# The general path of a ten-table embedding kernel: TensorE's 19 loop bodies become one loop over 199 tiles, and table 9 goes first

## The reference

```python
embs = [jnp.dot(x, w) for x, w in zip(xs, ws)]
emb_sum = embs[0]
q_emb = jnp.dot(xs[0] ** 2, ws[0] ** 2)
for i in range(1, len(xs)):
    emb_sum = emb_sum + embs[i]
    q_emb = q_emb + jnp.dot(xs[i] ** 2, ws[i] ** 2)
fm_ans = 0.5 * (emb_sum ** 2 - q_emb)
return jnp.concatenate([fm_ans] + embs, axis=-1)
```

## Time and profile before

| | us |
|---|---|
| median of 3 runs | 287.22 (287.17 to 287.44) |
| the profiled execution | 289.03 |
| its span | 287.3 |
| TensorE busy (matmul / weight load) | 218.8 / 154.5 |
| VectorE busy | 240.2 |
| ScalarE busy | 227.6 |
| GpSimd busy | 88.3 |
| moved by DMA | 113.90 MB, mean 396 GB/s |

### The profile page before, as it was taken

The page is one execution under the profiler, slowest core; times in us unless marked ns, Lnnn a source line. Parts: engine busy times, 40 slices in busy tenths (PEclk is TensorE's granted clock), DMA queues, the critical chain, the costliest instruction groups (busy, mean ns, idle before and its releaser), DMA issues.

```text
span 287.3 us, 2928 instructions
## 1 busy us (share of the span) xinstructions
PE 218.8 (76%) x878; PEld 154.5 (54%) x878; DVE 240.2 (84%) x236; ACT 227.6 (79%) x271; POOL 88.3 (31%) x68
## 2 busy tenths in 40 slices
PE   0459989999887888877887887887787888777760
PEld 0338757666555555555554554555555555555550
DVE  3742999999999998888889888988888898888960
ACT  0769999998987888788977877877877888787940
POOL 0442527326214304109224224314314304104000
PEclk9999999999999999999999999999999999999995
DMA  7999999999999999999999999999999999999932
GB/s 235 403 406 413 408 416 415 420 412 420 416 423 414 420 420 417 419 413 417 422 419 417 419 420 421 419 422 418 416 419 421 419 419 412 416 411 425 404 134 80
DMA packets 22419, 113.90 MB, mean 396 GB/s; under 512 B 3728, under 2 KB 4752, under 8 KB 10752
## 3 DMA queue, kind: packets, MB, share of 16 engines
q1 hardware_dynamic: 16976, 106.90, 90.5%
q10 hardware_dynamic: 5424, 6.79, 6.6%
HBM read 110.79 MB, written 2.88 MB: 396 GB/s over the span
## 4 chain that ended last, share of the span: by engine, by line
DMA 62%; issue 23%; DVE 6%; ACT 3%; PE 2%; POOL 1%; ACTq 1%; DVEq 0%; POOLq 0%
DMA x_ring<-in_x_dram 57%; DVE is_one L450 5%; DMA whole<-in_w_dram 5%; ACT is_set L287 2%; PE sums L376 1%; ACT turned L298 1%; POOL low L357 1%; PE sums L383 1%; DVE total L487 0%; ACT whole L280 0%; ACTq L267 0%; POOL high L355 0%; DVE results L490 0%; DVE results L493 0%; ACTq L274 0%
## 5 line engine op out<-in xcount | busy, mean ns | idle before, releaser
L450 DVE TENSOR_SCALAR_CACHE_REDUCE is_one<-x_ring 128x2048 uint8<-128x2048 f32 (+2 forms) x108 | 226.2, 2116 | 28.5 <-DMA x_ring<-in_x_dram 28.4
L287 ACT ACTIVATE is_set<-x_ring 128x2048 fp32r<-128x2048 uint32 (+2 forms) x108 | 192.1, 1783 | 37.1 <-DMA x_ring<-in_x_dram 37.0
L376 PE MATMUL sums<-is_set,low 128*128 128x512 f32 x398 | 135.3, 422 | 59.0 <-ACT is_set L287 52.2
L376 PE MATMUL sums<-is_set,high 128*128 128x512 f32 x398 | 126.2, 399 | 0.0
L376 PEld LDWEIGHTS sums<-is_set,low 128*128 128x128 f32 x398 | 68.7, 191 | 103.4 <-ACT is_set L287 53.8
L376 PEld LDWEIGHTS sums<-is_set,high 128*128 128x128 f32 x398 | 76.2, 191 | 17.8
L355 POOL CAST high<-whole 128x1024 fp32r<-128x1024 f32 (+5 forms) x31 | 27.0, 872 | 170.2 <-ACT whole L280 170.2
L357 POOL TENSOR_TENSOR low<-whole,high 128x1024 fp32r<-128x1024 f32 (+5 forms) x31 | 60.7, 1957 | 2.5
L287 ACT ACTIVATION_READ_ACCUMULATOR is_set<-x_ring 128x1 f32 (+1 forms) x108 | 20.6, 191 | 0.0
L280 ACT ACTIVATE whole<-whole 128x512 f32<-128x512 f32 (+5 forms) x31 | 16.7, 540 | 4.0 <-DMA whole<-in_w_dram 4.0
L383 PE MATMUL sums<-identity,turned 128*128 128x128 f32 x80 | 10.8, 280 | 0.8 <-ACT turned L328 0.8
(11 more groups left out here) (17 smaller groups left out, 3.7 us busy)
## 6 DMA issues: line engine op xcount, KB each, us to landing
x_ring<-in_x_dram SPq DMA_DIRECT2D x91, 1024.0 KB, 18.4
x_ring<-in_x_dram SPq DMA_DIRECT2D x16, 512.0 KB, 10.2
whole<-in_w_dram ACTq DMA_DIRECT2D x19, 256.0 KB, 7.4
out_dram<-results SPq DMA_DIRECT2D x10, 256.0 KB, 12.5
x_ring<-in_x_dram SPq DMA_DIRECT2D x1, 448.0 KB, 6.2
whole<-in_w_dram ACTq DMA_DIRECT2D x2, 192.0 KB, 5.6
whole<-in_w_dram ACTq DMA_DIRECT2D x2, 160.0 KB, 7.1
out_dram<-results ACTq DMA_DIRECT2D x1, 256.0 KB, 2.1
```

What stands on the lines that cost most here:

```text
L287: nc.scalar.activation(is_set[chunk.k % SETS][0:chunk.rows, 0:chunk.n * BATCH], x_of(chunk).bitcast(U32), ACT.Sign, accum_out=set_counts[0 ...
L376: last = nc.tensor.matmul(sums[:, summing(n, half), :], w, x[0:chunk.rows, at:at + HALF], start=first, stop=False, skip_group_check=True)
L450: nc.vector.tensor_scalar(is_one[chunk.k % 2][0:chunk.rows, 0:chunk.n * BATCH], x_of(chunk), 1.0, None, ALU.is_equal, ALU.add, accum_out=o ...
```

## The change

PE's general path becomes one loop over all 199 tiles, always with 128 rows. For that the last tile of a table with more than one is no longer cut to `TAIL` rows: SP loads the last 128 rows of `x` there (`x_end`, which overlaps the tile before), and places the weights so that the rows already done meet the zero rows of the padding; this takes one more DMA and one more wait on a new semaphore `gz_landed` in each of the nine tables. Table 9, with 112 rows and one tile, goes first, into a slot that DVE has set to zero, so that its missing rows are zero. DVE keeps its loops by table and works on 128 rows throughout. The usual path is as it was.

```diff
+G_ORDER = [9] + [t for t in range(NT) if t != 9]
...
-    x_tail = [x[P * (n - 1):P * (n - 1) + rows] for n, rows, x in zip(TILES, TAIL, xs)]
...
+        gz_landed = sem("gz_landed")
...
             with sp.If(odd != 0):
-                for t in range(NT):
-                    base = sum(TILES[:t])
-
-                    def load_tile(i, rows, x):
-
-                        sp.wait_ge(g_multiplied, base + i + 1)
-                        sp.dma_start(in_slot(0, BATCH)[0:rows], x).then_inc(gx_landed, 16)
-                        sp.dma_start(g_weights[:, 0, :], w_dram[t][:, bass.ds(i * D, D)]
-                                     ).then_inc(gw_landed, 16)
-
-                    if TILES[t] > 1:
-                        with sp.Fori(0, TILES[t] - 1) as i:
-                            load_tile(i, P, x_dram[t][:, bass.ds(i * BATCH, BATCH)])
-                    load_tile(TILES[t] - 1, TAIL[t], x_tail[t])
+                base = zeros = 0
+                for t in G_ORDER:
+                    end, rows = TILES[t] - 1, TAIL[t]
+                    if end:
+                        with sp.Fori(0, end) as i:
+
+                            sp.wait_ge(g_multiplied, base + i + 1)
+                            sp.dma_start(in_slot(0, BATCH), x_dram[t][:, bass.ds(i * BATCH, BATCH)]
+                                         ).then_inc(gx_landed, 16)
+                            sp.dma_start(g_weights[:, 0, :], w_dram[t][:, bass.ds(i * D, D)]
+                                         ).then_inc(gw_landed, 16)
+                    sp.wait_ge(g_multiplied, base + end + 1)
+                    sp.dma_start(in_slot(0, BATCH)[0:x_end[t].shape[0]], x_end[t]).then_inc(gx_landed, 16)
+                    w_end, before = w_dram[t][:, end * D:TILES[t] * D], P - rows if end else 0
+                    if before:
+
+                        sp.dma_start(g_weights[0:before, 0, :], w_end[rows:P]).then_inc(gz_landed, 16)
+                        zeros += 1
+                        sp.wait_ge(gz_landed, 16 * zeros)
+                    sp.dma_start(g_weights[before:P, 0, :], w_end[0:P - before]).then_inc(gw_landed, 16)
+                    base += TILES[t]
...
             with pe.If(odd != 0):
-                for t in range(NT):
-                    base = sum(TILES[:t])
-
-                    def multiply_tile(i, rows):
-                        pe.wait_ge(gx_landed, 16 * (base + i + 1))
-                        pe.wait_ge(gw_landed, 16 * (base + i + 1))
-                        pe.wait_ge(gx_ready, 2 * (base + i + 1))
-                        for b in range(NB):
...
-                    if TILES[t] > 1:
-                        with pe.Fori(0, TILES[t] - 1) as i:
-                            multiply_tile(i, P)
-                    multiply_tile(TILES[t] - 1, TAIL[t])
+                with pe.Fori(0, sum(TILES)) as i:
+                    pe.wait_ge(gx_landed, 16 * (i + 1))
+                    pe.wait_ge(gw_landed, 16 * (i + 1))
+                    pe.wait_ge(gx_ready, 2 * (i + 1))
+                    for b in range(NB):
+                        block_b = slice(b * P, (b + 1) * P)
+                        nc.tensor.matmul(sums[:, b, 0:D], in_slot(0, BATCH)[:, block_b],
+                                         g_weights[:, 0, :], start=True, stop=True,
+                                         skip_group_check=True)
+                        last = nc.tensor.matmul(sums[:, b, D:2 * D], in_slot(1, BATCH)[:, block_b],
+                                                g_weights[:, 1, :], start=False, stop=True,
+                                                skip_group_check=True)
+                    last.then_inc(g_multiplied, 1)
...
                 dve.wait_ge(x_multiplied, NCHUNKS)
+
+                g_link(nc.vector.memset(in_slot(0, BATCH), 0.0))
                 nc.vector.nop().then_inc(g_multiplied, 1)
...
-                for t in range(NT):
-                    base = sum(TILES[:t])
+                base = 0
+                for t in G_ORDER:
...
-                    def add_tile(i, rows):
+                    def add_tile(i):
...
-                            add_tile(i, P)
-                    add_tile(TILES[t] - 1, TAIL[t])
+                            add_tile(i)
+                    add_tile(TILES[t] - 1)
+                    base += TILES[t]
```

More of the change, by code:

```diff
@@ L507, in _ @@
                 dve.wait_ge(x_multiplied, NCHUNKS)
+                g_link(nc.vector.memset(in_slot(0, BATCH), 0.0))
                 nc.vector.nop().then_inc(g_multiplied, 1)
                 g_link(nc.vector.memset(total[:, :, :, :], 0.0))
-                for t in range(NT):
-                    base = sum(TILES[:t])
+                base = 0
+                for t in G_ORDER:
                     emb = results[:, t + 1, :, :]
                     g_link(nc.vector.memset(emb, 0.0))
-                    def add_tile(i, rows):
+                    def add_tile(i):
                         dve.wait_ge(gx_landed, 16 * (base + i + 1))
                         dve.wait_ge(gw_landed, 16 * (base + i + 1))
-                        x, w = in_slot(0, BATCH)[0:rows], g_weights[:, 0, :]
-                        nc.vector.tensor_tensor(in_slot(1, BATCH)[0:rows], x, x, ALU.mult
+                        x, w = in_slot(0, BATCH), g_weights[:, 0, :]
+                        nc.vector.tensor_tensor(in_slot(1, BATCH), x, x, ALU.mult
                                                 ).then_inc(gx_ready, 1)
```

## The result

The changed kernel takes 285.67 us (median of 5 runs, 285.48 to 286.18), the kernel before 287.44 us (5 runs, 287.17 to 287.58). The ratio is 0.9934, with a 95% interval of 0.9914 to 0.9954. It is faster, by 1.8 us or 0.7%. The prediction said 283.6 us, in a range of 282.8 to 284.8: the direction holds, the size is half of what was forecast, and the measured time lies above the range.

A forecast was written before the change was run, and what follows sets the result against it. DMA streaming bounds the body and PE's 5.18 us branch the end; PE gives back 4.6 us, but SP's drain comes next, so −3.6 us: 287.22 − 3.6 = 283.6 us, range 282.8 to 284.8 us.

The forecast's parts named there:

- What bounds, and what the change does: Whole kernel: streaming x untouched; only the tail differs, where PE's far branch waits 5.18 us for its program block.
- no change, because the stall is not bound to distance: PE's branch: its 5.18 us come from PE itself or memory is larger; time stays 287.2 us, chance 6%.
- PE's new cost: PE's branch at the end: jump over some 75 instructions, 0.05 to 0.07 us, drain at about 282.4 instead of 287.0.
- SP and DVE: Their branches at the end: slightly longer jumps into blocks fetched ahead, cost 0; SP drains last at 283.4 us.
- the rival on the other side: SP's branch at the end: its target falls out of the fetched code, time 288.3 us, slower; chance 4%.
- the conversion of the sum: From profiled execution to median: 289.03 − 3.6 = 285.4 us, less the same 1.8 us distance, gives 283.6 us.
- −3.6 us, the distance between the two drains: Block's end: PE's drain at 287.0 us gives way to SP's at 283.4 as the last, shortening the span 3.6 us.
- The upper end of the range: 284.8 us, from the rival that PE's near target is in a block still on its way, costing 2.6 us; chance 6%.

The follow-up runs named there:

- the 8 and 19 bodies: Changed kernel with PE's general path written out as 8 tile bodies (jump 525): 288.10 us, ratio 1.0029; as 19 bodies (jump 1,276): 287.42 us, ratio 0.9996.
- the 1 and 4: PE's general path as one loop body, the changed kernel itself (jump 70): 285.79 us when rerun; with 4 bodies (jump 265): 285.86 us, ratio 0.9962.
- The stretched jump of SP: Changed kernel with SP's never-run last stores written 18 times, so SP's branch jumps over 305 instructions instead of 118: 287.84 us, ratio 1.0007.
- the three usual profiles: Three more profiled executions of the unedited kernel before: 287.59, 287.53 and 287.82 us, with spans of 285.8, 285.7 and 286.0 us.

## Why the prediction was wrong

**What bounds, and what the change does: right.** The streaming is untouched, the tail after 280.9 us is all there is to win, PE's branch is its last piece, and its cost is a program fetch. The rival "no change, because the stall is not bound to distance" fell with the 8 and 19 bodies on one side and the 1 and 4 on the other (the profiled execution of 4). The Trainium skill, Runtime: NRT & Kernel Launch, section "Instruction fetch mechanics", has the same cause (a taken branch out of the resident blocks waits for a fetch), and the traces agree: 3.6 to 5.2 us here. PE's store of 2,048 instructions, which that section also gives, is not filled ahead: a target 525 instructions on was missing.

**PE's new cost: right where it counts.** Forecast a jump over about 75 and a drain at 282.4 us; the jump is over 70, the branch takes 0.23 us (0.1 was forecast, and the difference is hidden behind SP) and the drain starts at 282.2.

**SP and DVE: right.** SP's jump grew to 118 (forecast 121), DVE's to 163 (forecast 163), neither branch slowed, SP is last, at 283.7 us against a forecast 283.4. The stretched jump of SP shows that the rival on the other side was a real one, at half the price I gave it: 2.2 us more in place of up to 5.2, enough to cancel the gain and not enough to be measurably slower.

**The step that failed** is the conversion of the sum, as the prediction put it: "the median of the runs is 1.8 us below that execution, and I take the same distance". The term, "−3.6 us, the distance between the two drains", was right for that one execution. But most of the 1.8 us by which that execution exceeds the median sits in this very term: its stall was 5.18 us, the usual one is 3.76, which is 1.4 us less. (The rest is at least in part the median: 287.22 us was that of three runs, and the later lists of the kernel before have 287.38 to 287.68.) The prediction took the 1.8 us off the execution and still credited the median with the whole of the stall. In the three usual profiles the drains lie 2.0 to 2.1 us apart. That would have been 287.4 − 2.1 = 285.3 us, and measured were 285.67 and 285.79. Of the 0.4 to 0.5 us still between, part is that the changed kernel's two profiles reach L493 at 280.45 and 280.46 us and the three of before at 280.18 to 280.50; the rest is not resolved.

The first table of the profile had the warning in it: 289.03 us in the profiled execution beside three runs within 0.3 us of each other at 287.2. I took the 1.8 us for the profiler's, without a row that showed it. The upper end of the range should have come from the opposite reading, that the excess sits in the stall: 3.6 − 1.8 = 1.8 us, and 285.4 us.

## What to carry to other kernels

Where a profiled execution is longer than the runs by more than they differ among themselves, its excess sits somewhere in the trace; look for it first in a single long instruction, before a change is credited with all of that instruction. Code that never runs has a price where a branch must jump over it: keep a rarely used path as a short loop, so that the target stays in the block of the branch or the next one, and look at drains and branches line by line, since neither busy times nor the chain of waits show them. And what doesn't need to wait ahead of such a branch can wait behind it.

## What was not expected of the hardware

- A PE branch to code that isn't there took 3.6 to 4.0 us with one block of 16 KB fetched behind its start and 5.1 to 5.2 us with two, of which one then took 2.6 us in place of 1.1 to 1.5; 525 and 1,276 instructions cost the same.
- On PE that wait stands in the branch's own record. On SP it stands between the branch (0.045 us) and the next instruction: 2.7 us in place of 0.5.
- A satisfied wait instruction is recorded at 0.051 us on PE, but 244 in a row, which hold two waits each, took 26.6 us, 0.11 us for an instruction.
- PE's near branches are not free: 0.23 us over 70 instructions and 0.48 us over 265, against 0.07 us for DVE's over 163.
